# Gated linear attention with a SwiGLU-type network: K and Q spread over the partitions by DMA, outer products in the scan's layout, the sum over k partly in the centring matmul

## Chip, cores, metric

One Trainium2 chip, one core. The metric is the device time of one execution in microseconds (us). The kernel before takes 193.92 us (median of 3 runs, 193.89 to 194.09).

## What is computed

For x of 4 rows (b) of 512 tokens and 128 channels (16 heads of 8):

```
q, k, v = x@Wq, x@Wk, x@Wv            # as [head, 8] per token
gate = exp(log_sigmoid(x@Wgk1@Wgk2 + bgk2) / 16)
for t: state[h,v,k] = state[h,v,k]*gate[h,v] + v[h,v]*k[h,k];  o[h,v] = sum_k state[h,v,k]*q[h,k]
o = (normalise over channels(o) * gamma + beta) * silu(x@Wg);   x = layernorm(x + o@Wout)
h = silu(x@w1 * s1) * (x@w2 * s2);  h = gelu(h@h1 * s);  h = gelu(h@h2 * s);  x = layernorm(x + (h@w3 * s))
```

The first network layer is 128 to 512, the two hidden ones 512 to 512, the last 512 to 128. All is fp32.

## The kernel before, in words

A row of 512 tokens is one tile: channels (head, v) on the 128 partitions, tokens along the free dimension. The recurrence is one VectorE scan (L994) over 512 tokens for each k of 0 to 7, so eight scans for each row. The product v*k of every token is made with tokens on partitions (`u_tok`, 128x1024 for each of four token tiles; on GpSimd at L313, some on VectorE at L971), and TensorE turns it into the scan's layout with four transposes for each k (L515, `transpose_u`). Q of head h must stand on the 8 partitions of that head: TensorE replicates it with two matmuls for each k (L499 and L500, `replicate_q`). VectorE multiplies state and replicated q (L1005, `read_out`), GpSimd sums most products over k (L328), VectorE the last three (L1009, L1012). The sum is centred with one fp32 matmul (L526), and also transposed (L521) for the variance over channels (L1016, L1022); `o_rstd` is a power on GpSimd (L332). Then come `apply_gate` (L1050), `project_out` (L539), `add_x` (L1059), statistics, `r_rstd`, and four `x2_normalise` (L1028), which end the attention of a row. `x2` is transposed (L545) and rounded (L818), and the network of that row begins.

Matmuls with both operands large run in float32r: every operand is split into a rounded part (hi, made by ScalarE) and a rest (lo, made by VectorE at L1091 or GpSimd at L354). A flag, worked out on the chip from the weights' rests, skips the passes with the weights' lo parts: it is one value load and one branch of TensorE's program. In the profiled execution the short branch runs: of each weight block a hi pass (L591) and a rest pass (L600).

The order on each engine is written out by hand. After a prologue (projections of all four rows, attention of row 0) there are three periods: attention of row a beside the network of row a-1. Then the network of row 3 runs alone. The middle periods are a hardware loop of two iterations (`Fori`), the third has `follows` false at its end. On ScalarE a period has two activation table loads (Silu set L884, Gelu set L871). The SP queue issues all plain loads at the start (L255 to L270), in order, and later only the stores; the GpSimd queue issues the loads that round on the way (`w12_hi`, two `h_hi`, `w3_hi`, L387 to L390).

```
for k in range(3, DH):            # TensorE, row 0's attention among the projections
    transpose_u(0, k)
    replicate_q(0, k)
```

## Time and profile before

| | |
|---|---|
| median of 3 runs | 193.92 us |
| the profiled execution's own time | 193.71 us |
| its span, first to last instruction | 191.9 us |
| mean granted TensorE clock | 0.982 of 2.4 GHz |
| TensorE / VectorE / ScalarE / GpSimd busy | 162.0 / 147.9 / 117.5 / 113.8 us |
| bytes moved by DMA | 8.65 MB |

In the profile PE is TensorE's matmuls and PEld its weight loads, DVE is VectorE, ACT ScalarE, POOL GpSimd, SP the sync engine; a "q" behind a name is its queue. Busy time of PE is modelled: neighbouring matmuls overlap in it, and one matmul of 512 columns counts as 0.4 us where they follow one another every 0.23 us. Names in rows have no buffer number: att is any of att0 to att3.

### The profile page before, as it was taken

Reading aid. Unit: us, or ns where it says so; the run is one execution under the profiler, and the core shown is the slowest. Engines: PE = TensorE matmul, PEld = TensorE weight load, DVE = VectorE, ACT = ScalarE, POOL = GpSimd, SP = SyncE. Lnnn points to the kernel's source line nnn. Section 1 sums busy time; section 2 is a strip of 40 time slices with the busy share of each in tenths; the row PEclk is TensorE's granted clock in tenths of the full one; section 3 lists DMA queues with packets and bytes.
Section 4 is the critical chain, followed back from the end, with each engine's and each line's share of the span. In section 5 each row is a group of like instructions: output and inputs, shape, how many; then the busy total and the mean of one; then the engine's idle time right before and its main releaser. Section 6 shows DMA issues by size and latency. Waiting matters only on the chain.

```text
span 191.9 us, 2751 instructions
## 1 busy us (share of the span) xinstructions
PE 162.0 (84%) x790; PEld 124.0 (65%) x790; DVE 147.9 (77%) x301; ACT 117.5 (61%) x188; POOL 113.8 (59%) x94
## 2 busy tenths in 40 slices
PE   1859988969499997999999699999987999799840
PEld 1638656849387774878768487677856866567630
DVE  1398886988788997998999997899999685512360
ACT  4633649898037725378682556768454688979623
POOL 8989589919706689580677688427782313470011
PEclk9999999999979999999999999999999999999996
DMA  3999700000000000000000010000000100002002
GB/s 119 332 419 405 274 3 0 0 0 3 0 3 0 0 2 0 3 2 0 0 0 0 0 41 14 0 0 0 3 0 0 56 0 0 0 0 60 0 3 58
DMA packets 6191, 8.65 MB, mean 45 GB/s; under 512 B 513, under 2 KB 5026, under 8 KB 5666
## 3 DMA queue, kind: packets, MB, share of 16 engines
q1 hardware_dynamic: 5602, 5.60, 9.1%
q0 software_dynamic: 576, 2.88, 3.9%
q8 instruction: 7, 0.11, 0.3%
q14 instruction: 6, 0.05, 0.1%
HBM read 7.43 MB, written 1.05 MB: 44 GB/s over the span
## 4 chain that ended last, share of the span: by engine, by line
PE 25%; DVE 18%; issue 8%; ACT 5%; POOL 4%; DVEq 1%; POOLq 0%; ACTq 0%
PE ffn L600 8%; PE ffn L591 8%; DVE state L994 5%; DVE y L1005 2%; DVE y L1009 2%; DVE f_lo L1091 1%; ACT f_hi L831 1%; PE ffn L569 1%; DVE o_acc L1012 1%; DVE ffn L1080 1%; PE att L526 1%; POOL u_tok L313 1%; PE ffn L574 1%; ACT f_hi L839 1%; POOL o_rstd L332 1%
## 5 line engine op out<-in xcount | busy, mean ns | idle before, releaser
L354 POOL TENSOR_TENSOR f_lo<-full,f_hi 128x512 fp32r<-128x512 f32 x20 | 26.0, 1315 | 30.4 <-DVE full L1080 19.5
L994 DVE TENSOR_TENSOR_SCAN state<-gate,att 128x512 f32<-128x512 f32 x32 | 38.4, 1210 | 3.0 <-PE att L515 3.0
L839 ACT ACTIVATE f_hi<-ffn,vec_cols 128x512 fp32r<-128x512 f32 x32 | 22.1, 690 | 27.4 <-PE ffn L600 27.2
L591 PE MATMUL ffn<-f_hi,h_hi 128*128 128x512 f32 x128 | 36.7, 405 | 1.7 <-ACT f_hi L831 1.3
L600 PE MATMUL ffn<-f_lo,h_hi 128*128 128x512 f32 x128 | 35.6, 399 | 0.0
L591 PEld LDWEIGHTS ffn<-f_hi,h_hi 128*128 128x128 f32 x128 | 23.5, 188 | 8.7 <-ACT f_hi L831 3.0
L1091 DVE TENSOR_TENSOR f_lo<-ffn,f_hi 128x512 fp32r<-128x512 f32 x28 | 18.9, 687 | 12.4 <-ACT ffn L842 11.4
L600 PEld LDWEIGHTS ffn<-f_lo,h_hi 128*128 128x128 f32 x128 | 23.9, 188 | 5.8 <-DVE f_lo L1091 0.4
L313 POOL TENSOR_TENSOR u_tok<-kv_tok 128x1024 f32<-128x1024 f32 (+1 forms) x12 | 27.3, 2282 | 0.5 <-issue 0.4
L328 POOL TENSOR_TENSOR o_acc<-o_acc,y 128x512 f32<-128x512 f32 x16 | 20.6, 1290 | 7.9 <-DVE y L1005 7.8
L1005 DVE TENSOR_TENSOR y<-att,state 128x512 f32<-128x512 f32 x32 | 21.1, 671 | 0.0
L515 PE MATMUL att<-ident,u_tok 128*128 128x128 f32 x128 | 19.9, 292 | 0.0
L515 PEld LDWEIGHTS att<-ident,u_tok 128*128 128x128 f32 x128 | 16.8, 152 | 3.4 <-DVE state L994 1.2
L842 ACT ACTIVATE ffn<-ffn,vec_cols 128x512 f32<-128x512 f32 x24 | 15.9, 664 | 0.8
L499 PE MATMUL att<-q_hi,rep 128*128 128x512 f32 (+1 forms) x32 | 14.9, 465 | 0.7 <-DVE y L1005 0.7
L569 PE MATMUL ffn<-x_hi,w_hi 128*128 128x512 f32 x32 | 13.5, 423 | 1.0 <-DVE full L1080 0.7
L826 ACT ACTIVATE full<-ffn,vec_cols 128x512 f32<-128x512 f32 x16 | 11.0, 689 | 5.2 <-PE ffn L574 3.8
L574 PE MATMUL ffn<-x_lo,w_hi 128*128 128x512 f32 x32 | 12.8, 399 | 0.2 <-DVE x_lo L1074 0.2
L500 PE MATMUL att<-q_lo,rep 128*128 128x512 f32 (+1 forms) x32 | 12.6, 395 | 0.0
L1080 DVE SCALAR_TENSOR_TENSOR full<-ffn,vec_cols,full 128x512 f32<-128x512 f32 x12 | 8.7, 747 | 3.0 <-ACT full L826 2.8
L332 POOL TENSOR_TENSOR o_rstd<-o_var,half_neg 128x4 f32<-128x4 f32 x4 | 5.0, 1248 | 8.3 <-DVE o_var L1024 8.2
L415 POOL TENSOR_TENSOR e_rstd<-e_var,half_neg 128x2 f32<-128x2 f32 x2 | 1.4, 698 | 13.7 <-DVE e_minus L1258 13.7
(162 smaller groups left out, 318.6 us busy)
## 6 DMA issues: line engine op xcount, KB each, us to landing
h_raw<-in_hT SPq DMA_DIRECT2D x2, 1024.0 KB, 11.3
h_hi<-in_hT POOLq DMA_DIRECT2D x2, 1024.0 KB, 11.7
x_tok<-in_x SPq DMA_DIRECT2D x4, 256.0 KB, 5.0
out<-out_tok SPq DMA_DIRECT2D x3, 256.0 KB, 2.3
w_raw<-in_w12T SPq DMA_DIRECT2D x1, 512.0 KB, 4.6
w_hi<-in_w12T POOLq DMA_DIRECT2D x1, 512.0 KB, 8.1
xT_raw<-in_xT SPq DMA_DIRECT2D x1, 256.0 KB, 2.6
proj_raw<-in_proj SPq DMA_DIRECT2D x2, 128.0 KB, 2.3
```

The lines of the kernel that those rows point to most:

```text
L313: nc.gpsimd.tensor_tensor(u_tok[:, j].rearrange("p k (h v) -> p k h v", v=DH), v_b.unsqueeze(1).to_broadcast([P, DH, HEADS, DH]), k_b.unsq ...
L328: nc.gpsimd.tensor_tensor(o_acc[:], first, y[:, k % 4], ALU.add).then_inc(summed, 1)
L354: nc.gpsimd.tensor_tensor(lo[:, o], full_block(layer, o), hi[:, o].bitcast(F32), ALU.subtract).then_inc(pool_rested, 1)
L515: last = nc.tensor.transpose(A[2 + k % 2][:, tile(j)], u_tok[:, j, k], ident[:])
L569: nc.tensor.matmul(bank[:], w12_hi[:, n, tile(o)], x2_hi[:], start=True, stop=False)
L591: nc.tensor.matmul(bank[:], h_hi[:, layer - 1, c, tile(o)], src_hi[:, c], start=(c == 0), stop=False)
L600: last = nc.tensor.matmul(out_bank(layer, o)[:], h_hi[:, layer - 1, c, tile(o)], hidden[layer - 1][1][:, c], start=False, stop=(c == OB - 1))
L839: nc.scalar.activation(hidden[layer][0][:, o], bank[:], ACT.Gelu, scale=scales[:, 1 + layer, o:o + 1]).then_inc(gelu_hi_ready, 1)
L842: nc.scalar.activation(full_block(layer, o), bank[:], ACT.Gelu, scale=scales[:, 1 + layer, o:o + 1]).then_inc(gelu_ready, 1)
L994: nc.vector.tensor_tensor_scan(state[:, k % 3], gate[:, b], A[2 + k % 2][:], 0.0, ALU.mult, ALU.add).then_inc(scanned, 1)
L1005: nc.vector.tensor_tensor(y[:, k % 4], q_bank(b, k)[:], state[:, k % 3], ALU.mult).then_inc(y_ready, 1)
L1091: nc.vector.tensor_tensor(lo[:, o], full_block(layer, o), hi[:, o].bitcast(F32), ALU.subtract).then_inc(dve_rested, 1)
```

## The change

- K and Q are projected with channels on partitions, copied from PSUM (`keep_k`, `keep_q`), stored to DRAM (256 KB for each), and loaded back with every head's line repeated on its 8 partitions: four loads of 512 KB for K and four for Q in each row, each for two values of k, all on the SP queue and in a written order. V stays on chip (`v_own`).
- `outer_products(b, n)` on GpSimd multiplies `v_own` with two k of `k_rep` in the scan's layout, 128x1024; four for each row, all on GpSimd. `transpose_u`, `replicate_q`, `copy_kv`, `round_q`, `rest_of_q` and the outer products on VectorE go.
- The gate of the current row stands in a PSUM bank (`GATE`, placed by ScalarE), the states in two PSUM banks S; the scan reads gate from PSUM and u from SBUF and writes PSUM; `read_out` multiplies PSUM with `q_rep` in SBUF.
- `last_sums` and the transpose of o go: `center_o` is three accumulating fp32 matmuls (y6, y7, the sum of the rest). ScalarE squares the centred o, `variance_o` sums squares over channels with four one-column matmuls, `apply_gate` now waits for the squares.
- `x2_normalise` writes `x_tok`, `keep_x2` goes. It comes after `rest(f, 2, 3)` now; `transpose_x2` comes after `ffn_out_rest`.
- The loops are written out; weight loads, the weights' rests and the outputs' normalisation (`out_normalise`, in the last row between its second and third Gelu block) have other places in the order.

```diff
 # SP queue, after xT0, proj, gk, bias, x_tok 1..3, w12_raw, h_raw[:, 0]
+            def spread(dst, rows, n, loaded):
+                heads = rows[:, 2 * n * L:2 * (n + 1) * L].unsqueeze(1).to_broadcast([HEADS, DH, 2 * L])
+                sp.dma_start(dst[:, 2 * n:2 * n + 2].rearrange("p k t -> p (k t)"), heads).then_inc(loaded, 16)
+            def load_k(b, n):
+                sp.wait_ge(k_stored[b], 16)
+                if b >= 1:
+                    sp.wait_ge(u_ready, 4 * (b - 1) + n + 1)
+                spread(k_rep, k_rows[b], n, k_rep_loaded[n])
+            store_k(0)
+            load_k(0, 0)
+            load_k(0, 1)
+            store_q(0)
+            load_q(0, 0)
+            load_k(0, 2)
+            load_q(0, 1)
+            load_k(0, 3)
+            sp.dma_start(h_raw[:, 1], hT[:, 1]).then_inc(h2_loaded, 16)
+            load_q(0, 2)
+            load_q(0, 3)
             sp.dma_start(vec_cols[:], cols).then_inc(vecs_loaded, 16)
             sp.dma_start(wout[:], Wout).then_inc(wout_loaded, 16)
...
 # GpSimd
+            def outer_products(b, n):
+                pool.wait_ge(k_rep_loaded[n], 16 * (b + 1))
+                pool.wait_ge(v_kept, b + 1)
+                if b >= 1 or n >= 2:
+                    pool.wait_ge(scanned, DH * b + 2 * n - 2)
+                slot = 2 * (n % 2)
+                nc.gpsimd.tensor_tensor(u[:, slot:slot + 2], v_own[:, b].unsqueeze(1).to_broadcast([P, 2, L]),
+                                        k_rep[:, 2 * n:2 * n + 2], ALU.mult).then_inc(u_ready, 1)
+            weight_lo(0)
+            outer_products(0, 0)
+            outer_products(0, 1)
             pool.dma_start(h_hi[:, 1], hT[:, 1]).then_inc(h2_hi_loaded, 16)
             pool.dma_start(w3_hi[:], w3T).then_inc(w3_hi_loaded, 16)
             weight_lo(1)
+            outer_products(0, 2)
             sum_over_k(0, (1,))
+            outer_products(0, 3)
+            sum_over_k(0, (2,))
             weight_lo(2)
+            sum_over_k(0, (3,))
             weight_lo(3)
+            sum_over_k(0, (4, 5))
+            outer_products(1, 0)
             weight_lo(4)
+            o_rstd_of(0)
             weight_lo(5)
+            r_rstd_of(0)
+            outer_products(1, 1)
+            for a in range(1, B):
+                outer_products(a, 2)
+                rest(a - 1, 0, 0)
+                rest(a - 1, 0, 1)
+                rest(a - 1, 0, 2)
+                sum_over_k(a, (1,))
+                outer_products(a, 3)
+                rest(a - 1, 1, 0)
+                sum_over_k(a, (2,))
+                rest(a - 1, 1, 1)
+                sum_over_k(a, (3, 4, 5))
...
 # TensorE
             def center_o(b):
-                pe.wait_ge(o_ready, b + 1)
-                nc.tensor.matmul(A[3][:], center[:], o_acc[:], start=True, stop=True).then_inc(centered, 1)
+                pe.wait_ge(y_ready, DH * b + 7)
+                nc.tensor.matmul(T[:], center[:], y[:, 2], start=True, stop=False)
+                pe.wait_ge(y_ready, DH * b + 8)
+                nc.tensor.matmul(T[:], center[:], y[:, 3], start=False, stop=False)
+                pe.wait_ge(summed, (DH - 3) * (b + 1))
+                nc.tensor.matmul(T[:], center[:], o_acc[:], start=False, stop=True).then_inc(centered, 1)
+            def step(a, with_lo):
+                f = a - 1
+                for o in range(OB):
+                    ffn_hidden(f, 1, o, with_lo)
+                    ffn_hidden_rest(f, 1, o)
+                ffn_hidden(f, 2, 0, with_lo)
+                ffn_hidden_rest(f, 2, 0)
+                ffn_hidden(f, 2, 1, with_lo)
+                ffn_hidden_rest(f, 2, 1)
+                center_o(a)
+                ffn_hidden(f, 2, 2, with_lo)
+                variance_o(a)
+                project_out(a)
...
 # VectorE, a period
+            def period(a):
+                f = a - 1
+                ffn_product(f, 0)
+                ffn_product(f, 1)
+                if f >= 1:
+                    add_x2(f - 1)
+                ffn_product(f, 2)
+                scan(a, 2)
+                ffn_product(f, 3)
+                read_out(a, 1)
+                rest(f, 0, 3)
+                scan(a, 3)
+                read_out(a, 2)
+                if f >= 1:
+                    e_statistics(f - 1)
+                scan(a, 4)
+                read_out(a, 3)
+                scan(a, 5)
+                read_out(a, 4)
+                rest(f, 1, 2)
+                if f >= 1:
+                    e_mean_and_variance(f - 1)
+                scan(a, 6)
+                read_out(a, 5)
+                rest(f, 1, 3)
+                scan(a, 7)
+                read_out(a, 6)
+                read_out(a, 7)
+                rest(f, 2, 0)
+                rest(f, 2, 1)
+                apply_gate(a)
+                o_variance(a)
+                if a + 1 < B:
+                    scan(a + 1, 0)
+                add_x(a)
+                rest(f, 2, 2)
+                rest(f, 2, 3)
+                x2_normalise(a)
+                if a + 1 < B:
+                    scan(a + 1, 1)
+                rest_of_x2(a)
+                if a + 1 < B:
+                    read_out(a + 1, 0)
...
 # VectorE, between row 0's attention and the first period: add_beta_part(2), (3) now follow rest_of_x2(0)
```

## Rows read from the trace of the kernel before

**Rows 1.** The page: busy time and share, the granted clock in 40 slices.

```profile
PE 162.0 (84%) x790; PEld 124.0 (65%) x790; DVE 147.9 (77%) x301; ACT 117.5 (61%) x188; POOL 113.8 (59%) x94
...
PEclk9999999999979999999999999999999999999996
```

**Rows 2.** Timeline, the four x2_normalise of each row: start us, us.

```profile
49.83 1.36 DVE L1028 TENSOR_SCALAR x<-att,r_mv,r_rstd 128x128 f32<-128x128 f32 x4 [1.04 <-POOL r_rstd L332]
...
84.54 1.36 DVE L1028 TENSOR_SCALAR x<-att,r_mv,r_rstd 128x128 f32<-128x128 f32 x4
...
120.14 1.36 DVE L1028 TENSOR_SCALAR x<-att,r_mv,r_rstd 128x128 f32<-128x128 f32 x4
...
154.10 1.37 DVE L1028 TENSOR_SCALAR x<-att,r_mv,r_rstd 128x128 f32<-128x128 f32 x4
```

**Rows 3.** The chain that ended last, third period: start us, us, what.

```profile
131.46 0.60 ACT f_hi L831
...
144.96 1.13 PE att L526 x2
...
153.95 0.95 PE ffn L600 x4
...
156.65 0.59 ACT x_hi L818
```

**Rows 4.** Groups of instructions by line and shape, 92.07 to 127.47 us.

```profile
L994 DVE TENSOR_TENSOR_SCAN state<-gate,att 128x512 f32<-128x512 f32 x8 | 9.6, 1211 | 0.7 <-PE att L515 0.7
...
L313 POOL TENSOR_TENSOR u_tok<-kv_tok 128x1024 f32 x3 | 6.4, 2147 | 0.4 <-issue 0.4
...
L1005 DVE TENSOR_TENSOR y<-att,state 128x512 f32<-128x512 f32 x8 | 5.3, 673 | 0.0
L328 POOL TENSOR_TENSOR o_acc<-o_acc,y 128x512 f32<-128x512 f32 x4 | 5.2, 1290 | 2.5 <-DVE y L1005 2.5
...
L1009 DVE TENSOR_TENSOR y<-y 128x512 f32<-128x512 f32 x1 | 1.4, 1384 | 0.0
...
L1080 DVE SCALAR_TENSOR_TENSOR ffn<-ffn,vec_cols,full 128x512 f32<-128x512 f32 x1 | 0.7, 734 | 0.0
```

**Rows 5.** Timeline, turn into the third period.

```profile
122.00 0.59 ACT L818 CAST x_hi<-att 128x512 fp32r<-128x512 f32 x1 [1.06 <-PE att L545]
...
122.60 1.28 ACT L884 ACT_TABLE_LOAD   x1
```

**Rows 6.** Timeline of the prologue and of the branch behind it.

```profile
8.14 5.19 POOL L313 TENSOR_TENSOR u_tok<-kv_tok 128x1024 f32<-128x1024 f32 x2
...
17.43 2.33 DVE L994 TENSOR_TENSOR_SCAN state<-gate,att 128x512 f32<-128x512 f32 x2
...
22.86 2.38 POOL L361 TENSOR_TENSOR h_lo<-h_raw,h_hi 128x1024 fp32r<-128x1024 f32 x1
...
52.30 1.11 PE L545 MATMUL att<-ident,x 128*128 128x128 f32 x4 [2.68 <-issue]
...
56.31 0.69 ACT L826 ACTIVATE full<-ffn,vec_cols 128x512 f32<-128x512 f32 x1 [2.28 <-PE ffn L574]
```

**Rows 7.** DMA: the landing of h_raw's two loads, issues, and one stretch's rate.

```profile
L265 SPq DMA_DIRECT2D h_raw<-in_hT x1: 505/505/505, 5.4 to 5.4; - x1
...
DMA to landing us min/median/max: 7.8/11.3/14.8
...
out<-out_tok SPq DMA_DIRECT2D x3, 256.0 KB, 2.3
...
xT_raw<-in_xT SPq DMA_DIRECT2D x1, 256.0 KB, 2.6
...
12.00:14.00 2.00, 0.34 (x1) 0.34 (x2) 2.00 (x2) 1.34 (x3) 1.36 (x2) 1.00 1.32 422
```

**Rows 8.** Timeline of the last row: ScalarE's order behind the second Gelu layer.

```profile
173.47 1.65 ACT L853 ACTIVATE out_tok<-out_tok,e_shift,e_rstd 128x128 f32<-128x128 f32 x4
...
178.60 0.69 ACT L839 ACTIVATE f_hi<-ffn,vec_cols 128x512 fp32r<-128x512 f32 x1 [0.48 <-PE ffn L600]
```

More of the change, by code:

```diff
@@ new lines, in _ @@
+            load_k(1, 3)
+            load_q(1, 2)
+            load_q(1, 3)
+            store_k(2)
+            store_q(2)
+            store_k(3)
+            store_q(3)
+            for b in (2, 3):
+                load_k(b, 0)
+                load_k(b, 1)
+                load_q(b, 0)
+                load_k(b, 2)
+                load_q(b, 1)
+                load_k(b, 3)
+                load_q(b, 2)
+                load_q(b, 3)
+                if b == 3:
+                    store_out(0)
@@ L412, in _ @@
+            for o in range(3):
+                rest(B - 1, 0, o)
+            rest(B - 1, 1, 0)
+            rest(B - 1, 1, 1)
+            e_rstd_of(B - 2)
             for h in range(2):
@@ L747, in _ @@
-            transpose_o(0)
+            pe.wait_ge(k_kept, 3)
+            project_k(3)
+            pe.wait_ge(v_kept, 3)
+            project_v(3)
+            pe.wait_ge(q_kept, 3)
+            project_q(3)
+            project_beta(0)
+            pe.wait_ge(k_kept, 4)
+            project_g(1)
+            pe.wait_ge(v_kept, 4)
+            project_g(2)
+            project_beta(1)
+            pe.wait_ge(q_kept, 2)
             center_o(0)
-            project_beta(0)
-            project_q(3)
@@ L1217, in _ @@
             x2_normalise(0)
[L1218 to L1219 removed]
+            flag_exact()
+            scan(1, 1)
+            rest_of_x2(0)
             add_beta_part(2)
             add_beta_part(3)
[L1222 to L1224 removed]
             read_out(1, 0)
[L1226 to L1239 removed]
+            for a in range(1, B):
+                period(a)
+            last_row = B - 1
+            ffn_product(last_row, 0)
+            ffn_product(last_row, 1)
+            add_x2(last_row - 1)
+            ffn_product(last_row, 2)
+            ffn_product(last_row, 3)
+            rest(last_row, 0, 3)
+            e_statistics(last_row - 1)
+            e_mean_and_variance(last_row - 1)
             for layer in (1, 2):
```

724 lines of the change are left out of this document (267 added, 457 removed).

## The prediction

> **What bounds the kernel now.** I read the page first [rows 1]: TensorE is busy 84% of the span and VectorE 77%, so neither can be dropped from the argument, and GpSimd's 113.8 us are an average over stages. Then I cut the execution where a row's attention ends. Let X be the end of the four x2_normalise of a row: 51.2, 85.9, 121.5 and 155.5 us [rows 2]. So there is a prologue of 51.2, three periods of 34.7, 35.6 and 34.0, and a last part of 36.4, sum 191.9. In a period the groups by line [rows 4] show what TensorE gets rid of and what stays. The chain of waits [rows 3] shows which engine sets the end: in the first 23 us of a period it runs over VectorE (scans, products, sums over k), from the centring at 144.96 us to the last block behind 153.95 it is TensorE without a gap. The start [rows 6] has GpSimd with outer products from 8.1 us, and the first scans at 17.4.
>
> **The prologue.** K must now go to DRAM and back before the first outer product. SP's queue takes its transfers in order, and the store of K stands behind 2.8 MB, the last of it the first half of h_raw, which now lands at 13.2 us (issued 5.4, 7.8 to landing) [rows 7]. GpSimd's rounding loads start 4 us earlier in the changed kernel, and 1.5 MB of them stand before that point, about 0.6 MB more than now fits; at the 422 GB/s of [rows 7] that is 1.5 us, of which I take 1.2: 14.4. A store of 256 KB adds 0.65 for its bytes and some 0.8 for the landing (2.3 for an output store alone, with issue): 15.8. A load of 512 KB takes the 2.6 of the 256 KB load plus 0.65 for the other half: K is there at 19.1. Nearest row on either side: not before 17 (no wait behind GpSimd's loads), not after 23 (loads that read each line eight times at half the rate).
>
> From there GpSimd has work without a gap, in a fixed order: up to o_rstd it has five outer products, four weight rests of 1024 elements (2.38 each [rows 6]), five sums of 1.29 [rows 4], and two load issues of 0.55. The outer product reads two SBUF operands of 1024; its bounds are 2.15 (in the loop [rows 4]) and 2.6 (the first two, 5.19 for both [rows 6]); I take 2.3, near to the weight rest, whose operands are as plain. Sum 11.5 + 9.5 + 6.5 + 1.1 = 28.6, so 47.7. The other path ends later: ScalarE's last gate waits for the log_gate that VectorE does behind the fifth read_out, which waits for the third pair of Q. I put that pair at 35: from 22.5 us eight loads (4 MB with h_raw's second half ahead of the last two), shared with GpSimd's 1.25 MB. Behind the last gate come, in ScalarE's order, a table load, three silu, the fold of beta, three copies of row 3 and a rest's sum, some 8 us, and TensorE's centring waits for project_beta(1) behind them. It starts near 44 and is three fp32 matmuls instead of one: 1.13 for one [rows 3], 0.9 for each that follows, 2.9 in all. Square 0.6, gate 0.75, variance about 0.9 (four weight loads of squares and one column each; between 0.3 and one centring's 1.1) put o_var at 48.9. Then power 1.0, add_x 1.1, statistics 1.7, power 1.1, normalise 1.4: X0 = 55.5 with the hops, 4.3 later than now. Between bounds: 53 to 60.
>
> **The branch and the first period.** TensorE stood 2.68 us before 52.30 [rows 6]; that stays, as flag and branch do. But in the changed order VectorE does two add_beta (1.3) behind rest_of_x2, and ffn_in waits for all four. The first Silu, now at X0 + 5.1 (56.31 [rows 6]), comes at X0 + 5.5 though eight transposes and a replication before it are gone. Then the same count as below without the last row's sums gives 34.7, as now.
>
> **A middle period**, counted from X. ScalarE rounds x2 by 1.1 (it ended at X + 1.1 where TensorE was free; 122.59 is X + 1.1 [rows 5]), loads the table 1.28 and scales y: 3.1; that cover hides scan, rest and read_out of the next row on VectorE. Four Silu/product/round steps end at 9.3; now they end at 10.6 (132.06 [rows 3]), because TensorE no longer makes transposes and replications in between. From there VectorE is the chain: six scans have started or follow at 1.12 (2.33 for two [rows 6]), products at 0.6 (0.67 less the overlap [rows 4]), rests likewise, statistics 0.9 and 0.7. The last read_out ends at 22.2. GpSimd ends the fifth sum at 21.4 (sum, outer product, rest, sum, rest, three sums from 9.4, 1.29 and 2.3 each, with 0.6 of waits), so it is late next: the loads for it are long there, as each waits only for work of the row before. Gone are the outer product, the two late additions (1.38 for the first beside GpSimd [rows 4]) and one set of statistics, 5 us of VectorE's work; two rests and the last aggregation moved ahead of the last scans take 1.9 of that back. TensorE loses 32 transposes and 16 replications (some 3.7 each at 0.23 for 512 columns, 0.95 for four [rows 3]) but has nothing to put there: it waits 1.6 for rest(1, 3) and has its second block done at 22.1.
>
> Centring then ends at 25.0 (2.9). Square 25.7 and gate 26.55 now stand in series; behind them variance, project_out and 1.9 + 0.9 for the rest of block 2 and block 3: 30.4. Two Gelu passes to 31.9, rest 32.65, and only then the normalise: X + 34.0. The other way, variance 26.7, scan(a+1, 0), power, add_x, statistics, power, ends at 32.0. So 34.0 in place of 35.6; the third period, 33.9 in place of 34.0, since x2 now waits for the network's last rest where it ran beside it.
>
> **Prices no row shows.** A scan with its gate and result in PSUM: VectorE's product that writes PSUM takes 0.734, hardly less than its like in SBUF, and read_out takes PSUM and SBUF in 0.673 [rows 4], so I take 1.12 as now; bounds 1.0 and 1.4, that is -1 to +2 us for a row. Unrolled loops: 0, between -0.5 and +1. Square and place_gate on ScalarE, 0.6 each, lie in its waits for TensorE.
>
> **The last part.** Rounding of x2 comes 0.7 sooner after X (1.1 against 1.8, 157.24 [rows 3]), but out_normalise, 1.65, now stands between the second and third Gelu block [rows 8] where ScalarE has 0.5 of slack for each block: +0.7. So 36.4 stays.
>
> **Sum:** 55.5 + 34.7 + 34.0 + 33.9 + 36.4 = 194.5 of span against 191.9. The profiled execution's own time is 193.7, 1.8 more than its span, and 0.2 below the median: 194.5 + 2.0 = 196.5 us, 1.3% slower. A difference under 0.2% cannot be told from none here.
>
> **A rule weighed.** The additions with two SBUF operands took 1.38 beside GpSimd; read_out, with one in PSUM, did not grow over its 0.673 [rows 4]. [...]
>
> **The rivals.** (1) Faster, 0.33: the relief of TensorE reaches the path. Its place is the second half of a period: if rest(1, 3) and the centring do not hold TensorE up, the end comes 1.6 to 2 us sooner each time, periods of 32.5 each, and 55.5 + 97.5 + 36.4 + 2.0 = 191.4. For it: 12 us of TensorE's work leave each period in busy terms and VectorE has under 29 left. Against it: the chain of waits is VectorE's up to the centring, and a longer centring, square and a later normalise are added behind it. It decides when the three periods sum to under 100.0, or X0 comes before 53. (2) Much slower, 0.17: the replicating loads run at half the rate. Row 0's eight take 20 us instead of 10, the last pair of Q lands near 46, X0 near 62, and the time is 203. Against it: the loads' lines are 4 KB and the queue gave 422 GB/s. (3) No difference, 0.05: the prologue's loss of 4.3 against periods at 33.2, 193.9. My forecast itself: 0.45.
>
> **Numbers.** Slower 0.45 + 0.17 = 0.62, same 0.05, faster 0.33. The range leaves out the tails of both rivals: 190 to 202; the likeliest case alone is 194.3 to 199.
>
> **What would show it.** Right: k_rep's first load lands at 18 to 21 us, first scan near 21.5 (17.4 now), X0 at 54 to 57, middle period near 34, scan at 1.2, TensorE busy down by 30 to 40 us without the time following, GpSimd up by 5 to 8. Wrong: first scan before 19; periods under 33; a scan over 1.3; or TensorE's granted clock low in the prologue, where it now waits more (it fell after the 2.7 us wait at the branch [rows 1]), which would lengthen centring and projections there.

## The result and the profile after

The changed kernel takes 218.45 us (median of 4 runs, 217.25 to 218.57), the kernel before, on the same chip, 194.00 (median of 4): ratio of the means (218.18 and 194.55; one of the four runs before took 196.31) 1.121, 95% interval 1.112 to 1.131. It is 12.1% slower. The forecast was 196.5 us, range 190 to 202, so the sign was right and the size was not; the range did not hold the time. The profiled execution took 218.42 us, its span 216.6.

The page of the changed kernel (busy time, granted clock, DMA share and GB/s in 40 slices), beside [rows 1]:

```profile
PE 155.1 (72%) x606; PEld 109.4 (51%) x606; DVE 127.3 (59%) x253; ACT 117.4 (54%) x190; POOL 118.6 (55%) x95
...
PEclk9999857556979758999999999999997998899996
DMA  5985599986499850786230777010000001000101
GB/s 171 358 344 146 163 253 309 320 227 172 145 234 239 288 138 2 198 225 185 73 89 8 193 194 197 3 48 0 0 0 0 3 0 50 0 2 0 34 21 51
```

Every engine but GpSimd has less or as much to do, and the span is 25 us longer: the time is in waits, and in work of TensorE at a low clock. A slice is 5.4 us. The DMA engines are close to full from 27 to 49 us and again from 60 to 76. The granted clock is low in most slices from 27 to 54 us and again in the one from 76.

The timeline's four x2_normalise (start, duration), beside [rows 2], show where the time went:

```profile
71.27 1.37 DVE L1037 TENSOR_SCALAR x_tok<-state,r_mv,r_rstd 128x128 f32<-128x128 f32 x4 [0.45 <-POOL r_rstd L375]
...
108.54 1.36 DVE L1037 TENSOR_SCALAR x_tok<-state,r_mv,r_rstd 128x128 f32<-128x128 f32 x4
...
142.22 1.36 DVE L1037 TENSOR_SCALAR x_tok<-state,r_mv,r_rstd 128x128 f32<-128x128 f32 x4
...
178.63 1.36 DVE L1037 TENSOR_SCALAR x_tok<-state,r_mv,r_rstd 128x128 f32<-128x128 f32 x4
```

| | before | forecast | after | after - forecast |
|---|---|---|---|---|
| prologue, X0 | 51.2 | 55.5 | 72.64 | +17.1 |
| first period | 34.7 | 34.7 | 37.26 | +2.6 |
| middle period | 35.6 | 34.0 | 33.68 | -0.3 |
| third period | 34.0 | 33.9 | 36.41 | +2.5 |
| last part | 36.4 | 36.4 | 36.61 | +0.2 |

The prologue carries 17.1 of the 22.1 us by which the span was missed; 2.6 and 2.5 lie in the first and third period.

**The prologue.** From the chain of waits up to the fifth read_out (start, duration, what):

```profile
8.90 8.11 DMA k_rows<-kq_own
...
17.02 0.64 SPq L270
...
27.81 17.27 DMA q_rep<-q_rows
...
45.10 0.69 DVE y L989
```

K's store lands at 17.01 (forecast 15.8), the first load of k_rep at 22.1 (19.1). The third pair of Q, issued at 27.81, lands at 45.1; the forecast put it at 35. VectorE stands for it 7.13 us, with six scans and four read_outs done. ScalarE's timeline behind that (in brackets the idle time before, and what ended it) shows a second wait:

```profile
46.42 0.63 ACT L788 ACTIVATE gate<-gate 128x512 f32<-128x512 f32 x1 [8.20 <-DVE gate L963]
...
56.70 0.59 ACT L770 COPY kq_own<-ffn 128x512 f32<-128x512 f32 x1 [5.43 <-DMA q_rows<-kq_own]
...
64.31 0.60 ACT L799 ACTIVATE o_sq<-att 128x512 f32<-128x512 f32 x1 [4.48 <-PE att L514]
```

keep_q(3) copies row 3's Q into the slot that row 1's Q had, and waits for that one's store (q_stored[1]). SP issues that store only at 50.14, since row 1's first two loads of K stand ahead of it in the queue's order, and they wait for the store of row 1's K: issued at 32.30, behind row 0's loads and the weights, it lands 16.6 us later, at 48.9. SP's waits from 30 to 60 us (us in total, times, longest):

```profile
SPq L270 <- DMA k_rows<-kq_own: 8.9, 1, 8.9
SPq L270 <- DMA q_rows<-kq_own: 5.8, 1, 5.8
```

The store of Q lands at 56.6. The silu that the projections of beta need are behind this copy, so TensorE stands 4.44 us and then runs at the lower of its two clocks: of the three centring matmuls (two passes each) the first takes 1.92 us, the last 1.02:

```profile
58.88 1.89 PE L526 MATMUL ffn<-wout_beta,silu_g 128*128 128x128 f32 x8 [4.44 <-ACT silu_g L803]
60.56 1.92 PE L510 MATMUL att<-y,center 128*128 128x512 f32 x2
...
63.26 1.02 PE L514 MATMUL att<-o_acc,center 128*128 128x512 f32 x2
```

The DMA issues (KB each, median us from issue to landing), where [rows 7] had 2.6 and 2.3 for 256 KB:

```profile
k_rep<-k_rows SPq DMA_DIRECT2D x16, 512.0 KB, 6.1
q_rep<-q_rows SPq DMA_DIRECT2D x16, 512.0 KB, 5.3
...
k_rows<-kq_own SPq DMA_DIRECT2D x4, 256.0 KB, 11.3
```

**The middle period** went as forecast in its parts: the last read_out ends at X + 22.0 (forecast 22.2), centring at X + 24.7 (25.0). The prices too: scans at 1.222 with gate and result in PSUM (1.211 in [rows 4], and taken as unchanged), read_out 0.672. GpSimd's outer product, forecast at 2.3, takes 2.378:

```profile
L358 POOL TENSOR_TENSOR u<-v_own,k_rep 128x1024 f32<-128x1024 f32 x5 | 11.9, 2378 | 1.8 <-DVE state L976 1.8
L976 DVE TENSOR_TENSOR_SCAN state<-gate_now,u 128x512 f32<-128x512 f32 x8 | 9.8, 1222 | 0.2
...
L989 DVE TENSOR_TENSOR y<-state,q_rep 128x512 f32<-128x512 f32 x8 | 5.3, 672 | 0.0
```

### The profile page after: what moved, and what is told of

It reads as the page before. It is cut to its first block, busy times and chain, and to the rows that moved or that the text cites. A ratio compares the mean times of both kernels' runs of the same rounds, so it can differ in the third digit from the quotient of the medians.

```text
span 216.6 us, 2106 instructions
## 1 busy us (share of the span) xinstructions
PE 155.1 (72%) x606; PEld 109.4 (51%) x606; DVE 127.3 (59%) x253; ACT 117.4 (54%) x190; POOL 118.6 (55%) x95
## 4 chain that ended last, share of the span: by engine, by line
PE 33%; DVE 19%; DMA 16%; issue 13%; ACT 11%; POOL 4%; SPq 3%; ACTq 0%; POOLq 0%; DVEq 0%
PE ffn L594 9%; DMA q_rep<-q_rows 8%; PE ffn L585 8%; DVE state L976 6%; DMA k_rows<-kq_own 4%; DVE y L989 3%; DMA q_rows<-kq_own 3%; DVE f_lo L1059 3%; PE ffn L563 3%; PE ffn L568 2%; ACT f_hi L835 2%; PE att L539 2%; ACT ffn L838 2%; SPq L270 2%; DMA bias_row<-in_bias 2%
## 5 line engine op out<-in xcount | busy, mean ns | idle before, releaser
L358 POOL TENSOR_TENSOR u<-v_own,k_rep 128x1024 f32<-128x1024 f32 x16 | 37.9, 2368 | 18.9 <-DMA k_rep<-k_rows 14.1
L585 PE MATMUL ffn<-f_hi,h_hi 128*128 128x512 f32 x128 | 39.5, 421 | 7.2 <-ACT f_hi L827 5.7
L976 DVE TENSOR_TENSOR_SCAN state<-gate_now,u 128x512 f32<-128x512 f32 x32 | 39.1, 1224 | 8.0 <-POOL u L358 7.2
L594 PE MATMUL ffn<-f_lo,h_hi 128*128 128x512 f32 x128 | 37.2, 409 | 4.1 <-DVE f_lo L1059 4.1
L585 PEld LDWEIGHTS ffn<-f_hi,h_hi 128*128 128x128 f32 x128 | 24.1, 191 | 18.0 <-ACT f_hi L827 8.5
L1059 DVE TENSOR_TENSOR f_lo<-ffn,f_hi 128x512 fp32r<-128x512 f32 x28 | 19.2, 687 | 19.1 <-ACT ffn L838 18.2
L989 DVE TENSOR_TENSOR y<-state,q_rep 128x512 f32<-128x512 f32 x32 | 21.3, 675 | 9.7 <-DMA q_rep<-q_rows 9.7
L371 POOL TENSOR_TENSOR o_acc<-o_acc,y 128x512 f32<-128x512 f32 x16 | 20.5, 1284 | 1.3 <-DVE y L989 0.4
L563 PE MATMUL ffn<-x_hi,w_hi 128*128 128x512 f32 x32 | 15.9, 497 | 5.1 <-DVE x_tok L1011 2.7
L466 PE MATMUL ffn<-x_hi,proj_hi 128*128 128x512 f32 x17 | 9.8, 578 | 10.2 <-DVE gate L963 10.2
L568 PE MATMUL ffn<-x_lo,w_hi 128*128 128x512 f32 x32 | 15.2, 475 | 0.9 <-DVE x_lo L1042 0.9
L563 PEld LDWEIGHTS ffn<-x_hi,w_hi 128*128 128x128 f32 x32 | 7.2, 226 | 8.6 <-issue 3.1
L1019 DVE SCALAR_TENSOR_TENSOR og<-att,vec_cols,silu_g 128x512 f32<-128x512 f32 x4 | 3.0, 751 | 14.5 <-ACT o_sq L799 14.5
L466 PEld LDWEIGHTS ffn<-x_hi,proj_hi 128*128 128x128 f32 x17 | 4.4, 262 | 13.2 <-DVE gate L963 10.6
```

What stands on the lines that cost most here:

```text
L358: nc.gpsimd.tensor_tensor(u[:, slot:slot + 2], v_own[:, b].unsqueeze(1).to_broadcast([P, 2, L]), k_rep[:, 2 * n:2 * n + 2], ALU.mult).then ...
L371: nc.gpsimd.tensor_tensor(o_acc[:], first, y[:, k % 4], ALU.add).then_inc(summed, 1)
L563: nc.tensor.matmul(bank[:], w12_hi[:, n, tile(o)], x2_hi[:], start=True, stop=False)
L568: nc.tensor.matmul(bank[:], w12_hi[:, n, tile(o)], x2_lo[:], start=False, stop=True).then_inc(ready, 1)
L585: nc.tensor.matmul(bank[:], h_hi[:, layer - 1, c, tile(o)], src_hi[:, c], start=(c == 0), stop=False)
L594: last = nc.tensor.matmul(out_bank(layer, o)[:], h_hi[:, layer - 1, c, tile(o)], hidden[layer - 1][1][:, c], start=False, stop=(c == OB - 1))
```

## The experiments

Each run is one profiled execution of the changed kernel with the edit shown; e10_combined was timed in rounds as well. X0 is the end of the prologue, the periods run between the ends of x2_normalise.

| kernel | us | X0 | periods |
|---|---|---|---|
| changed | 218.4 | 72.6 | 37.3, 33.7, 36.4 |
| e1_own_q3 | 210.9 | 66.2 | 37.0, 35.1, 34.7 |
| e2_distinct | 209.1 | 63.3 | 37.2, 34.9, 35.2 |
| e3_warm | 216.0 | 73.2 | 37.2, 33.7, 33.7 |
| e4_early | 216.9 | 73.2 | 36.6, 34.8, 34.5 |
| e5_repeat_hT | 218.5 | 72.3 | 37.3, 36.4, 34.7 |
| e6_stores_first | 212.0 | 64.7 | 36.5, 37.7, 34.9 |
| e7_early_stores | 211.0 | 64.3 | 37.2, 36.4, 34.8 |
| e8_e_stats_late | 217.1 | 73.5 | 36.5, 34.0, 34.1 |
| e9_own_q3_distinct | 202.4 | 58.1 | 36.9, 34.9, 34.6 |
| e10_combined | 208.1 | 63.6 | 37.0, 34.2, 34.2 |
| e11_beta_first | 217.5 | 75.1 | 35.2, 35.1, 34.7 |
| e12_beta_first_warm | 216.3 | 74.3 | 34.7, 35.0, 34.7 |

Kernels that leave the prologue's work alone have X0 from 72.3 to 75.1, so of X0 less than 3 us is not read as an effect.

### The wait for the stores of row 1

```diff
-                    .dma_start(q_rows[b]..., kq_own[:, 2 * (b % 2) + 1]).then_inc(q_stored[b], 16)
+                    .dma_start(q_rows[b]..., kq_own[:, 2 * (b % 2) + 1] if b < 3 else full[:, 2]).then_inc(q_stored[b], 16)
...
-                if b >= 2:
+                if b == 2:
                     act.wait_ge(q_stored[b - 2], 16)
```

The copy itself goes to the same block full[:, 2], and ScalarE waits for q_stored[3] before it writes that block in the first period.

> The changed kernel with a buffer of its own for row 3's Q, so that ScalarE's copy of it no longer waits for the store of row 1's Q. Theory 1 (ScalarE is held from 51.3 to 56.7 us by that wait, and beta's part, centring and square queue behind it): the squares come 4 to 5.5 us sooner, X0 at 67 to 69 instead of 72.6, the time near 214. Rival (centring is late anyway, behind the sums or GpSimd's rests): less than 1 us.

Measured: 210.85 us, X0 66.2. ScalarE's timeline:

```profile
51.83 0.58 ACT L770 COPY full<-ffn 128x512 f32<-128x512 f32 x1 [0.33 <-PE ffn L470]
...
57.84 0.60 ACT L799 ACTIVATE o_sq<-att 128x512 f32<-128x512 f32 x1 [2.82 <-PE att L514]
```

The copy comes 4.9 us sooner and the squares 6.5, X0 as much. The third pair of Q lands as late as before (45.3). So the wait is a cause by itself, and larger than I gave it (4 to 5.5 us for the squares, 214 us for the time). Of the 6.5 us 4.9 are the wait. The other 1.6 lie between the copy and the squares, 7.6 us in the changed kernel and 6.0 here, where TensorE does not come back at its lower clock: the three centring matmuls take 2.7 us instead of 3.7. The other way to take it away is to issue the stores sooner:

```diff
             load_k(0, 3)
+            store_k(1)
+            store_q(1)
             sp.dma_start(h_raw[:, 1], hT[:, 1]).then_inc(h2_loaded, 16)
...
-            store_k(1)
             load_k(1, 0)
             load_k(1, 1)
-            store_q(1)
```

> Only SP's order changes: row 1's K and Q are stored ahead of the second h_raw load and of row 0's last two loads of Q, so that no copy waits for a store. Theory 1: ScalarE is free as with the buffer of its own, X0 at 66 to 68 (72.6 before), time 210 to 213, a little of it lost because Q's third pair comes 1 to 2 us later. Rival (the gain of e1 came from something else in that run): under 2 us.

Measured: 212.04 us, X0 64.7; keep_q(3) starts at 50.37 without a wait. The order of two 256 KB stores on a queue was worth 8 us of prologue. (The second period of this run is long for the reason given further down.)

### The rate of the replicating loads

```diff
-    heads = rows[:, 2 * n * L:2 * (n + 1) * L].unsqueeze(1).to_broadcast([HEADS, DH, 2 * L])
+    heads = hT[:, n // 2, 2 * (n % 2):2 * (n % 2) + 2].rearrange("p a d -> p (a d)")
```

> The loads into k_rep and q_rep read 128 different lines of 4 KB of a weight tensor instead of every line eight times; same bytes, same number, same waits (the numbers computed are not the reference's: K and Q are replaced by weights). Theory 2 (reading a line eight times is what makes these loads slow, 230 to 300 GB/s where the weights came at 400): the third pair of Q lands at 38 to 40 us instead of 45.1, X0 3 to 6 us sooner, time 212 to 215. Rival (the engines move any such mixture of loads at this rate, or the queue's order and the round trips set it): landing times within 1 us, time 217.5 to 219.

Measured: 209.08 us, X0 63.3. The loads of q_rep in the changed kernel, then in this one (duration of the issue, min, median, max in ns; under it the time to landing in us):

```profile
L270 SPq DMA_DIRECT2D q_rep<-q_rows x16: 514/515/1967, 24.6 to 132.0; - x16
...
DMA to landing us min/median/max: 4.2/5.3/17.3
```

```profile
L270 SPq DMA_DIRECT2D q_rep<-in_hT x16: 327/328/670, 22.6 to 123.8; - x16
...
DMA to landing us min/median/max: 3.3/3.6/13.1
```

And the stretches (last two columns: DMA share, GB/s) of changed kernel, then e2_distinct:

```profile
24.00:32.00 8.00, 1.63 (x3) 0.98 (x4) 5.32 (x6) 0.63 (x1) 6.39 (x6) 0.56 0.70 198
32.00:40.00 8.00, 4.24 (x12) 2.95 (x11) 5.51 (x7) 4.96 (x9) 4.79 (x3) 0.71 1.13 333
```

```profile
24.00:32.00 8.00, 4.54 (x10) 3.23 (x11) 7.39 (x10) 2.28 (x4) 7.99 (x6) 0.60 1.01 370
32.00:40.00 8.00, 2.31 (x7) 1.59 (x7) 4.75 (x6) 4.21 (x9) 8.00 (x6) 0.71 1.05 389
```

Same bytes in the same number of packets, 370 and 389 GB/s instead of 198 and 333 (in the second stretch of the changed kernel the weights' plain loads are mixed in). The first stretch is not a fair pair: six of row 0's eight loads are issued from 24.59 us on in the changed kernel and from 22.64 in this one, so its DMA share is 0.70 there. In stretches of 2 us in which the share is 1 or near it, the changed kernel moves 246 to 314 GB/s between 30 and 48 us, one stretch of 409 apart, and e2_distinct 342 to 418 between 24 and 40; plain loads are mixed into both. The third pair of Q lands at 37.8 instead of 45.1, and X0 comes 9.3 us sooner, where I had expected 3 to 6. Is it the repeated line or the place it is read from (a DRAM tensor written just before)? The next kernel reads the weights, but repeats each line eight times:

```diff
-    heads = rows[:, 2 * n * L:2 * (n + 1) * L].unsqueeze(1).to_broadcast([HEADS, DH, 2 * L])
+    heads = hT[0:HEADS, n // 2, 2 * (n % 2):2 * (n % 2) + 2].rearrange("p a d -> p (a d)").unsqueeze(1).to_broadcast([HEADS, DH, 2 * L])
```

> The loads into k_rep and q_rep read 16 lines of the weight tensor, each for 8 partitions, instead of 16 lines of the K or Q just stored (the numbers computed are not the reference's). Theory 2 (repeating a line is what slows them, wherever it lies): as in the changed kernel, medians of 5 to 6 us to landing, third pair of Q at 44 to 46 us, time 216 to 219. Rival (it is the region, small and just written): as with distinct lines, 3.6 to 4.2 us to landing, third pair near 37.8, time near 209.

Measured: 218.5 us, X0 72.3; the third pair of Q lands at 44.0, and rates and landings are near those of the changed kernel (medians 6.0 us for K and 4.7 for Q, where it had 6.1 and 5.3):

```profile
L270 SPq DMA_DIRECT2D q_rep<-in_hT x16: 536/540/697, 24.3 to 132.8; - x16
...
DMA to landing us min/median/max: 4.4/4.7/17.5
```

The repetition is the cause. Even the issue on SP takes 0.54 us instead of 0.33.

### Both at once

Edit: those of e1_own_q3 and e2_distinct together.

> Both causes of the late prologue taken away at once: row 3's Q goes to a block that is still free, so that ScalarE waits for no store of row 1's Q, and the replicating loads read 128 distinct 4 KB lines of the weights hT instead of each line of K and Q eight times (so K and Q in the scan are not the reference's). Alone they moved the end of the prologue from 72.6 to 66.2 us and to 63.3 us. If they are two parts of one chain (late third pair of Q, then the keeping wait) and GpSimd's own work stands close behind, the gains do not add: by GpSimd's order (own_q3: squares' sums and row 1's outer products around 55, rest 57.4, 1/rms 59.8) the prologue ends at 58 to 62 and the kernel takes 203 to 207. If they are independent the gains add: 72.6 - 6.5 - 9.3 = 56.8, near the forecast's 55.5, and the time is 200 to 203. If only one of the two matters once the other is gone: 63 again, 208 to 209. Periods 37, 34.5, 34.5 as in those two runs.

Measured: 202.41 us, X0 58.1 (56.69 and 1.37). The gains were 6.5 and 9.3 alone and are 14.6 together, 1.2 less than their sum and between the two cases of the expectation. From the timelines:

```profile
37.65 0.69 DVE L991 TENSOR_TENSOR y<-state,q_rep 128x512 f32<-128x512 f32 x1 [3.10 <-DMA q_rep<-in_hT]
...
49.72 0.60 ACT L799 ACTIVATE o_sq<-att 128x512 f32<-128x512 f32 x1 [2.82 <-PE att L514]
...
51.70 1.03 POOL L375 TENSOR_TENSOR o_rstd<-o_var,half_neg 128x4 f32<-128x4 f32 x1 [1.57 <-DVE o_var L1006]
...
56.69 1.37 DVE L1039 TENSOR_SCALAR x_tok<-state,r_mv,r_rstd 128x128 f32<-128x128 f32 x4 [0.45 <-POOL r_rstd L375]
```

That lies within the bounds of the prologue that I had worked out (55.5, between 53 and 60), once the two things that I had wrong in it are taken away. The 2.6 us that are left are there already when the third pair of Q lands, at 37.65 against 35: the squares start at 49.7 against 46.9, and from o_var on the steps take what the forecast gave them. GpSimd is not the bound in this run: it stands 1.57 us before o_rstd and waits for o_var. The time, 202.4 us, is even so above the range: the first period is still 2.2 us over its forecast, the other two together 1.6.

### Was it the clock, or the weights ahead of K?

TensorE's granted clock was 0.5 to 0.7 from 27 to 54 us. The next kernel gives TensorE 44 matmuls behind project_q(2) and 20 behind project_g(2), whose results nobody reads.

```diff
             project_q(2)
+            pe.wait_ge(q_kept, 2)
+            for _ in range(44):
+                nc.tensor.matmul(T[:], proj_hi[:, 0], x_hi[:, 0], start=True, stop=True)
             pe.wait_ge(z_log_ready, 4)
```

> Extra matmuls without use fill TensorE's two long waits of the prologue (44 before it waits for the last log_gate, 20 before beta's part of row 1). Theory 3 (part of the loss is TensorE's granted clock of 0.5 after these waits): the projections at 46 us run at 0.23 us instead of 0.43, centring takes 2.7 instead of 3.7 us, X0 2 to 3.5 us sooner, time 215 to 216. Rival (these matmuls were covered by ScalarE's wait for the store): under 1 us, time 217.5 to 218.5.

Measured: 215.98 us, but X0 73.2. The prologue as a whole gained nothing. The projections that got faster stood in front of ScalarE's wait, and the 44 matmuls held them up until 50.8 us; the copy behind the wait starts at 58.89, 2.2 us later than in the changed kernel. Behind it the faster centring did help: the squares start 5.95 us behind the copy (64.84) instead of 7.61. The 2.4 us by which the total fell came in the third period (33.7 instead of 36.4), which the edit does not touch; the reason is below. The total lies in the range that I expected (215 to 216) by luck, and alone would have been read as a success.

The next moves row 0's stores and loads of K and Q ahead of the feed-forward weights, and GpSimd's remainders behind the sums.

```diff
-            sp.dma_start(w12_raw[:], w12T).then_inc(w12_loaded, 16)
-            sp.dma_start(h_raw[:, 0], hT[:, 0]).then_inc(h1_loaded, 16)
...
             store_k(0)
             load_k(0, 0)
...
-            sp.dma_start(h_raw[:, 1], hT[:, 1]).then_inc(h2_loaded, 16)
             load_q(0, 2)
             load_q(0, 3)
...
+            sp.dma_start(w12_raw[:], w12T).then_inc(w12_loaded, 16)
+            sp.dma_start(h_raw[:, 0], hT[:, 0]).then_inc(h1_loaded, 16)
+            sp.dma_start(h_raw[:, 1], hT[:, 1]).then_inc(h2_loaded, 16)
```

> K and Q of row 0 go ahead of the weights: w12, both h and the rounding loads are issued behind row 0's replicated loads, and the weights' rests and their sums come later in GpSimd's and ScalarE's order. Theory 4 (the order of the queues makes row 0 late): K lands near 13 instead of 22, first scan near 15.5 instead of 24.5, third pair of Q near 27 instead of 45, X0 6 to 12 us sooner, time 206 to 212. Rival (the bytes before X0 and GpSimd's rests set X0 whatever the order): first scan early but X0 within 3 us of 72.6.

Measured: 216.91 us, X0 73.2, though the first scan starts at 21.05 instead of 24.45 and the last read_out ends at 38.8 instead of 50.6. K is there at 14.4, near the 13 expected, but the scan, expected at 15.5, stands on VectorE behind an x_lo that waits for ScalarE's rounding until 20.44. The rival of the expectation (X0 within 3 us) held. ScalarE's timeline:

```profile
48.38 0.59 ACT L761 COPY kq_own<-ffn 128x512 f32<-128x512 f32 x1 [10.76 <-DMA k_rows<-kq_own]
...
56.24 0.59 ACT L771 COPY kq_own<-ffn 128x512 f32<-128x512 f32 x1 [6.79 <-DMA q_rows<-kq_own]
```

The attention's eight steps are done 12 us earlier, and the same store holds the same copy until 56.2: all of the gain is given back there. With that wait gone as well (row 1's stores also ahead of the weights):

> Row 0's K and Q ahead of the weights as in e4, and the stores of row 1 behind them but ahead of the weights, so that ScalarE's copies wait for nothing. Theory 4 with theory 1 (e4 gained nothing because its copies of K and Q of row 3 waited until 48.4 and 56.2 us for stores behind 3 MB of weights): centring near 42 instead of 60, X0 at 56 to 62, time 200 to 206. Rival (the weights' bytes and GpSimd's rests of the weights bound X0 then): X0 at 64 or later, time over 208.

Measured: 211.02 us, X0 64.3; here too the rival of the expectation held (X0 at 64 or later, over 208 us). VectorE's timeline shows what took its place:

```profile
51.57 0.69 DVE L1012 TENSOR_TENSOR x_tok<-ffn,x_tok 128x512 f32<-128x512 f32 x1 [13.87 <-DMA x_tok<-in_x]
...
59.14 1.14 DVE L1029 SCALAR_TENSOR_TENSOR state<-state,o_rstd,x_tok 128x128 f32<-128x128 f32 x4 [2.14 <-POOL o_rstd L374]
```

x_tok of row 0, the last load of the queue, arrives at 51.5. GpSimd stands until 53.4 for row 1's first load of K, and behind that outer product and one more remainder it comes to o_rstd at 58.0, though o_var was there at 53.0. None of the orders tried gets under 63 with the replicating loads as they are: what is moved forward pushes something else back.

### The third period

```diff
                 rest(f, 1, 2)
-                if f >= 1:
-                    e_mean_and_variance(f - 1)
...
                 rest(f, 2, 1)
+                if f >= 1:
+                    e_mean_and_variance(f - 1)
                 apply_gate(a)
```

In the changed kernel's third period a four-column instruction of VectorE, with operands in SBUF, starts at the same time as GpSimd's two sums and lasts until the first of them ends; a rest is late behind it, TensorE stands 2.45 us and comes back at the lower clock (L585 x4 1.86 us, 1.09 at 157.8). First the same place in the middle period, where it took 0.15 us, then the third:

```profile
127.14 0.15 DVE L1073 TENSOR_SCALAR e_minus<-e_mv 128x4 f32<-128x4 f32 x1
...
160.44 0.50 DVE L1000 TENSOR_SCALAR e_var<-e_mv 128x4 f32<-128x4 f32 x1
...
160.85 1.33 DVE L1073 TENSOR_SCALAR e_minus<-e_mv 128x4 f32<-128x4 f32 x1
160.86 2.70 POOL L371 TENSOR_TENSOR o_acc<-o_acc,y 128x512 f32<-128x512 f32 x2
...
164.54 0.50 PE L594 MATMUL ffn<-f_lo,h_hi 128*128 128x512 f32 x1 [2.45 <-DVE f_lo L1059]
...
164.88 1.86 PE L585 MATMUL ffn<-f_hi,h_hi 128*128 128x512 f32 x4
```

> The output's mean and variance move behind rest(f, 2, 1), out of the stretch where GpSimd sums without a pause. Theory 5 (in the third period two operations on 4 columns took 0.50 and 1.33 us because GpSimd held the SBUF port, the last scans came 1.8 us late, TensorE waited 2.45 us for rest(1, 3) and its clock fell): no such operation over 0.3 us, no wait over 2 us there, third period 33.5 to 34.7 instead of 36.4, time 215.5 to 217. Rival (the clock falls for another reason): third period stays over 36.

Measured: 217.12 us, periods 34.0 and 34.1. VectorE's timeline:

```profile
168.94 0.17 DVE L1000 TENSOR_SCALAR e_var<-e_mv 128x4 f32<-128x4 f32 x1
169.02 0.16 DVE L1073 TENSOR_SCALAR e_minus<-e_mv 128x4 f32<-128x4 f32 x1
```

The other runs say the same without having been made for it. In eleven kernels the statistics stand where the change has them, so there are 22 middle and third periods: in four of them e_minus took 1.33, and these are the four long ones (36.4, 36.4, 36.4, 37.7); in the other 18 it took 0.15 or 0.16, and they last 33.7 to 35.2. What decides whether it is hit is not shown. By the traces e_minus starts 0.01 to 0.03 us ahead of a sum of GpSimd in 21 of the 22 periods, the four long ones among them (in the middle period above the sums start at 127.16), so its place beside the sum is not enough. That the hit falls on another period, or on none, in kernels whose edit lies in the prologue fits a difference of timing too small for these traces. e_var, the four-column instruction just before, took 0.49 to 0.52 us in 21 of the 22 (GpSimd made a remainder beside it) and 0.17 in e8_e_stats_late. In the remaining period of the 22 (the middle one of e2_distinct) neither was held for long (0.19 and 0.15).

### The first period

```diff
-            scan(1, 1)
-            rest_of_x2(0)
             add_beta_part(2)
             add_beta_part(3)
+            rest_of_x2(0)
+            scan(1, 1)
             read_out(1, 0)
```

TensorE in the changed kernel behind X0 = 72.64:

```profile
73.78 1.11 PE L539 MATMUL att<-ident,x_tok 128*128 128x128 f32 x4 [2.47 <-issue]
77.58 0.77 PE L563 MATMUL ffn<-x_hi,w_hi 128*128 128x512 f32 x1 [2.69 <-DVE x_tok L1011]
```

> On the first period alone (37.3 us, forecast 34.7). In the changed kernel the first matmul of the feed-forward network starts 4.94 us behind X0, since it waits (2.69 us) for the last two add_beta, which VectorE does only behind a scan and rest_of_x2; and the 16 matmuls behind it run at 0.43 us each, granted clock 0.50, until 83.1. Edit: VectorE does the two add_beta right behind the flag, and the scan after rest_of_x2. Theory: the wait is the first part of the loss; ffn_in starts at X0 + 3.1, TensorE's wait there falls from 2.7 to about 0.7 us, the clock stays at 0.50 at first as TensorE still stood 2.5 us before the transposes, and the first period is 35.0 to 36.0 us; time 216.5 to 217.5. Rival: the period is set by VectorE's scans and GpSimd, which get nothing from it: period 37, time 218.4. X0 stays at 72.6 and the other periods at 33.7 and 34.5 to 36.4.

Measured: 217.47 us, first period 35.2 instead of 37.3, the network's first matmul 2.9 us behind X0 instead of 4.9. X0 itself was 75.1 in this run, for an edit that lies behind it; so the total says little and the period is what counts. With work for TensorE in the wait for the flag:

```diff
             count_lo()
+            for _ in range(8):
+                nc.tensor.matmul(T[:], proj_hi[:, 0], x_hi[:, 0], start=True, stop=True)
             pe.wait_ge(exact_ready, 1)
```

> The edit of beta_first and besides eight matmuls into a free bank, whose result nobody reads, in TensorE's 2.5 us of waiting for the flag. Theory: the low clock is the second part of the loss; with work there and a short wait behind it the granted clock stays at 1.00, the 16 matmuls of ffn_in take 0.23 us each instead of 0.43, 3 us less, and the first period comes to 33.5 to 34.5 us, the forecast's 34.7 or under; time 214.5 to 216. Rival: the clock is low there for another reason (DMA traffic or what came before), or the matmuls only shift the branch: period as in beta_first.

Measured: 216.28 us, first period 34.7. The clock still fell (0.50 from 74 to 77) but was back when the network's matmuls came, 0.23 us apart:

```profile
75.61 1.06 PE L539 MATMUL att<-ident,x_tok 128*128 128x128 f32 x4
...
78.40 0.40 PE L563 MATMUL ffn<-x_hi,w_hi 128*128 128x512 f32 x1
78.63 0.40 PE L568 MATMUL ffn<-x_lo,w_hi 128*128 128x512 f32 x1
```

So of the 2.6 us too many 2.1 went with the late additions of beta; the 0.5 that the work in the wait added is less than the 0.8 by which the first periods of the other kernels differ (36.5 to 37.3), and the clock was expected to be worth 1 to 2. The split holds for this order of the two edits alone. In the kernel before the same matmuls started 4.5 us behind X0 (55.65), only 0.5 sooner than in the changed one; what differed more was their pace, 0.43 us apart for twelve of them instead of 0.23, which is 2.4 us by my estimate. Started at X0 + 2.9, they had the clock back at X0 + 6.8, in the changed kernel at X0 + 10.2. The share of the clock when both are there is not separated by this.

### A version of all that helps

Row 3's K and Q in slots of their own, h_raw's second half behind row 0's loads of Q, o_rstd ahead of the fifth remainder, the statistics of e8_e_stats_late:

```diff
-        kq_own = sb("kq_own", [P, 4, L])
+        kq_own = sb("kq_own", [P, 6, L])
+        OWN = (0, 2, 0, 4)
...
             load_q(0, 2)
             load_q(0, 3)
+            sp.dma_start(h_raw[:, 1], hT[:, 1]).then_inc(h2_loaded, 16)
...
-            weight_lo(4)
             o_rstd_of(0)
+            weight_lo(4)
```

> What the runs pointed to, put together in a kernel that computes what the reference does: row 3's K and Q have slots of their own (ScalarE waits for no store of row 1), h_raw's second half is loaded after the last two pairs of row 0's Q, GpSimd makes row 0's 1/rms before the fifth remainder of the weights, and e's mean and variance come after the third remainder of the layer, clear of GpSimd's 2.7 us sum. Theory: prologue ends at 62 to 65 instead of 72.6, first period 36 to 37, the others 34.0 to 34.7: 206 to 209 us, 4 to 6% under the changed kernel and still 6 to 8% over the kernel before, since the replicating loads keep their slow rate and the outer products on GpSimd stay. Rival: GpSimd's order is then the bound and only own_q3's gain shows: 210 to 211.

Measured: 208.13 us (median of 4, 206.49 to 208.52), 194.26 for the kernel before (median of 7), ratio of the means 1.069 with an interval of 1.063 to 1.076. X0 63.6, periods 37.0, 34.2, 34.2. It is 4.7% under the changed kernel and 6.9% over the kernel before. Even with the first period of e12_beta_first_warm it would be near 206; the kernel before stays the best.

## Why the prediction was wrong

**What held.** Slower, as said. The middle period (34.0 forecast, 33.7; 34.0 where the statistics stand clear), the last part (36.4, 36.6) and the scan and read_out from PSUM (1.22, 0.67) came within 0.3 us. Rival 1, the relief of TensorE reaching the path, is refuted: periods add up to 107.4, and in the best run to 104.3, never under 100. One of the numbers that were to show my case was poor: TensorE's busy time fell by 6.9 us, not by 30 to 40. The transposes and replications went, but the centring matmuls came, and in the prologue the granted clock was 0.72 in the mean from the first scan to X0, which makes the rest longer. (A low clock there was one of the signs that I had named for being wrong.) The 12 us per period that I gave rival 1 as TensorE's relief are 4.6 in the middle period (33.41 to 28.84 us of busy time, by the stretches between the X). GpSimd's rose by 4.8 (5 to 8 said), VectorE's fell by 20.6.

**The step that failed first: "I put that pair at 35".** It rested on 422 GB/s, a rate of loads that read each line once [rows 7]. Loads that read each line eight times ran at 246 to 314 GB/s with the engines full, where distinct ones had 342 to 418, and landed 5.3 us behind issue (median of Q) where those took 3.6. The pair came at 45.1; with distinct lines it came at 37.8, so 2.8 of the 10 us are not the repetition, and no run says what they are. This was my rival 2, in its mechanism and its first number ("near 46"), and I gave it 0.17: the 4 KB lines and the queue's rate, which I held against it, say nothing of repetition, for which no row of before speaks. The experiments put its worth at 9.3 us of X0 (8.1 on top of the other edit). "K is there at 19.1" came at 22.1, of which 1.2 is the store and 1.8 the first load; distinct lines take 1.1 of the 1.8 back (GpSimd starts 3.9 us behind the issue in e2_distinct, 5.1 in the changed kernel). The Trainium skill, page DMA: Bandwidth & Descriptors, on its two cost components, gives about 2.0 us plus the bytes at 436 GB/s for a DMA that GpSimd issues. Taken over to this store, which SP issues, that is an estimate of 2.6 us and a landing at 17.0. It landed at 17.01, but that is luck: the trace does not bear out the parts. The first half of h_raw ahead of it, issued at 7.54, took 8.9 us and landed at 16.4, where I had 14.4; the store was there 0.6 us behind it, where I gave 1.4 and the estimate 2.6. Alone at the head of the queue in e4_early it took 2.0.

**The step that was missing: "three copies of row 3 and a rest's sum, some 8 us".** I counted the instructions in ScalarE's order and not what they wait for. keep_k and keep_q of row b wait for the stores of row b - 2, since kq_own has four slots; the store of row 1's Q stands on SP behind two loads that wait for the store of row 1's K, which stands in turn behind 16.6 us of queue. From the end of the last gate (47.05) to the end of the silu that TensorE waits for (58.84) ScalarE took 11.8 us; without the wait, in e1_own_q3, 6.7 (47.28 to 54.0). Two edits that take the wait away by different means gave 6.5 and 7.9 us. The change adds this wait, and I did not ask who queues behind it. Rival 2's X0, "near 62", lies below what the slow loads alone give: 66.2 in e1_own_q3, 64.7 with the stores first.

The two together explain 14.6 of the 17.1 us. The rest, 58.1 against 55.5, is the third pair of Q at 37.65 instead of 35, with distinct lines too; from there to X0 the forecast gave 20.5 us and e9_own_q3_distinct took 20.4.

**First period, 34.7 as now.** I wrote that ffn_in waits for all four additions of beta and gave that no time, since the first Silu came only 0.4 later in my count. In fact the matmuls started 4.9 us behind X0, and at half the clock: in the kernel before, the transposes and replications that the change takes out had stood between the branch and ffn_in, and the granted clock, 0.50 from 52 to 54 us, was 1.00 from 56 us on, when the network's matmuls ran. What was "gone" had given TensorE work there; that this brought its clock back is read from the two traces, not tested. Moving the additions gave back 2.1, and with work in the wait besides the period was the forecast's 34.7.

**Third period, 33.9.** Lengthened to 36.4 by a 0.16 us instruction that took 1.33 beside GpSimd's sum. In the kernel before, it took 0.16 each time, in a stretch in which GpSimd made no sum. I had asked only whether the large instructions are slowed beside GpSimd. Scans and read_outs, each with an operand in PSUM, were not (1.22 and 0.67). The Trainium skill, page SBUF — State Buffer, under "Who interferes with whom", says the same of an instruction with at most one SBUF input outside the two-port modes, and the trace agrees; but it also counts tensor_scalar among those that can run in a two-port mode and then contend with GpSimd. The price of the short one was not its own 1.2 us: TensorE's wait and the low clock after it made it 2.4.

**The range.** It ended at 202, with 0.17 for the one case near it. The right case was slower by two causes that add, and each alone was outside (210.9 and 209.1 us with the other taken away). Even with both away the run took 202.4, so the 2.6 us of the prologue and the 3.8 of the three periods that came late besides would have passed the upper end by themselves.

## What to carry to other kernels

A load that spreads one line of DRAM over several partitions moves the same bytes as a plain one and took here about 1.5 times as long from issue to landing (medians): price it by such a load, and where none is in the trace, take the slow end as likely. Of every wait that a change adds, follow both sides, what stands behind the waiting instruction on its engine and what stands ahead of the releasing one on its queue; two stores of 256 KB in a late place of the queue cost 8 us here. And compare periods, not totals: in several of these runs the total moved by 2 us for a reason that was not in the edit.

## What the runs showed of the hardware that was not expected

- Loads that repeat each 4 KB line eight times: landing 6.1 and 5.3 us (K, Q) against 4.2 and 3.6 for 128 distinct lines of the same size, whether they come from a fresh DRAM tensor or from a weight; their issue on SP took 0.51 to 0.55 us against 0.33 to 0.38.
- A TENSOR_SCALAR of four columns, SBUF to SBUF, took 1.33 us beside GpSimd's sum of two SBUF operands in 4 periods, and 0.15 or 0.16 in 17 others in which it started as close ahead of that sum (0.01 to 0.03 us). The rule of contention quoted above from the Trainium skill, page SBUF — State Buffer, would fit the four, but no run here varied the operands of that instruction, and none shows what spared the others; only its place was tried.
- Two stretches with the same idle time (2.68 us before the transposes in [rows 6], 2.47 after the change) both brought the clock to 0.50. In the kernel before it was back at 1.00 by 56 us, 3.7 us after the work resumed; in the changed kernel, where TensorE stood another 2.69 us in between, only at about 82.8, 9.0 us after.
